# A graph attention layer on one core: the mish ratio moves from PSUM to SBUF, and the fourth tile of four groups goes through TensorE

## The reference

```python
sent   = nodes[senders] @ Ws + bs
e_att  = sent + edges @ We + be
recv   = nodes[receivers] @ Wr + br
logits = sum over a head of mish(e_att + recv) * attn_w + attn_b      # mish(x) = x * tanh(softplus(x))
w      = softmax of logits over the edges of one receiver
out    = segment_sum(w * e_att, receivers)
x      = layernorm(x + out)
```

## Time and profile before

| | |
|---|---|
| median of 3 runs | 3876.78 us (3872.36 to 3880.77) |
| the profiled execution | 3882.45 us, its span 3880.6 us |
| mean granted TensorE clock | 0.747 |
| busy: PE, DVE, ACT, POOL | 1900.8, 1878.8, 1681.8, 1552.4 us |

### The profile page before, as it was taken

The page is one execution under the profiler, slowest core; times in us unless marked ns, Lnnn a source line. Parts: engine busy times, 40 slices in busy tenths (PEclk is TensorE's granted clock), DMA queues, the critical chain, the costliest instruction groups (busy, mean ns, idle before and its releaser), DMA issues.

```text
span 3880.6 us, 49688 instructions
## 1 busy us (share of the span) xinstructions
PE 1900.8 (49%) x15454; PEld 1818.1 (47%) x15454; DVE 1878.8 (48%) x4399; ACT 1681.8 (43%) x2921; POOL 1552.4 (40%) x1640
## 2 busy tenths in 40 slices
PE   3345534544553553454364355356445445435536
PEld 3345534533543553454354355355445445435536
DVE  2435544544543554454465355445445445445537
ACT  0335534533543453453354354345335445435435
POOL 3443353344344334334434434433433543443440
PEclk8777777876876787787677677677668777767868
DMA  6111221211211121121121212212112112111220
GB/s 183 54 57 47 75 61 49 74 58 54 69 58 58 46 76 58 52 72 58 54 71 56 58 51 73 58 49 75 58 52 71 59 56 71 58 56 47 76 59 10
DMA packets 107469, 240.31 MB, mean 62 GB/s; under 512 B 46429, under 2 KB 73300, under 8 KB 100412
## 3 DMA queue, kind: packets, MB, share of 16 engines
q0 software_dynamic: 52224, 107.06, 10.5%
q1 hardware_dynamic: 53074, 132.41, 9.9%
q10 hardware_dynamic: 2142, 0.49, 0.1%
HBM read 230.09 MB, written 9.74 MB: 62 GB/s over the span
## 4 chain that ended last, share of the span: by engine, by line
another core or an unknown queue 32%; PE 26%; issue 21%; DVE 17%; ACT 1%; ACTq 1%; DVEq 1%
PE ps_z L785 7%; PE ps_z L786 6%; PE ps_sum L819 6%; DVE tbuf L1163 3%; DVE tbuf L1142 3%; DVE Z L1124 3%; DVE onehot L1113 2%; PE ps_edgeT L766 2%; DVE tbuf L1135 2%; PE ps_onehotT L771 2%; PE ps_ends L808 2%; PE ps_ends L800 1%; DVE Z L1232 1%; PE ps_ends L827 1%
## 5 line engine op out<-in xcount | busy, mean ns | idle before, releaser
L694 POOL DMA_INDIRECT gath<-xs_table,src_i x1632 | 1551.4, 951 | 2234.7 <-DVE Z L1124 1239.6
L785 PE MATMUL ps_z<-we_sb,edgeT 128*128 128x128 f32 x3264 | 722.5, 307 | 1545.7 <-ACT edgeT L909 888.2
L785 PEld LDWEIGHTS ps_z<-we_sb,edgeT 128*128 128x128 f32 x3264 | 564.8, 217 | 1569.6 <-ACT edgeT L909 904.0
L1124 DVE TENSOR_TENSOR Z<-ps_z,gath 128x512 f32<-128x512 f32 x408 | 280.9, 688 | 1616.5 <-remote 1076.6
L909 ACT COPY edgeT<-ps_edgeT 128x512 f32<-128x512 f32 x408 | 238.7, 585 | 1550.8 <-remote 1390.9
L786 PE MATMUL ps_z<-xr_buf,onehotT 128*128 128x128 f32 x3264 | 705.3, 302 | 0.0
L786 PEld LDWEIGHTS ps_z<-xr_buf,onehotT 128*128 128x128 f32 x3264 | 568.9, 218 | 0.0
L819 PE MATMUL ps_sum<-Z,onehot 128*128 128x132 f32 x3264 | 446.2, 286 | 17.0 <-issue 12.5
L819 PEld LDWEIGHTS ps_sum<-Z,onehot 128*128 128x128 f32 x3264 | 403.3, 195 | 15.3 <-issue 10.6
L940 ACT ACTIVATE ps_ratio<-tbuf,c_ln 128x512 f32<-128x512 f32 x408 | 281.8, 691 | 188.8 <-issue 120.3
L916 ACT CAST onehotT<-ps_onehotT 128x512 f32<-128x512 bf16 x408 | 240.6, 590 | 247.9 <-remote 122.0
(11 more groups left out here) (113 smaller groups left out, 1695.0 us busy)
## 6 DMA issues: line engine op xcount, KB each, us to landing
edge_buf<-in_edge_attr_dram SPq DMA_DIRECT2D x51, 2048.0 KB, 7.9
gath<-xs_table,src_i POOLq DMA_INDIRECT x1632
xr_buf<-xr_table SPq DMA_DIRECT2D x51, 64.0 KB
xr_in<-xr_table SPq DMA_DIRECT2D x51, 64.0 KB
x_in<-in_x_dram SPq DMA_DIRECT2D x51, 64.0 KB
out_dram<-y_out SPq DMA_DIRECT2D x51, 64.0 KB, 1.6
xs_table<-onehot SPq DMA_DIRECT2D x2, 896.0 KB
xr_table<-Z SPq DMA_DIRECT2D x1, 1568.0 KB
```

The source lines that it names most:

```text
L694: nc.gpsimd.indirect_dma_start(gath[:, b, t, :], None, xs_dram, bass.IndirectOffsetOnAxis(ap=src_i[:, b, t:t + 1], axis=0))\
L785: nc.tensor.matmul(ps_z[q][:, j, :], edgeT[:, q, j, :], we_sb[:, :], start=True, stop=False)
L1124: nc.vector.tensor_tensor(Zv[:, b, a:a + n, 0:D], ps_z[g % 2][:, 0:n, :], gath[:, b, a:a + n, :], ALU.add).then_inc(z_ready, 1)
```

## The change

The ratio's last step writes in place to tbuf in SBUF, and its wait for the mish before goes. The bank that this frees takes the heads' logits, so that ps_ends can hold four transposed tiles. TURN_T becomes 4: all tiles of the turned groups go through PE, 16 of 32. `score` and `reduce_heads` are left out for the turned groups, and their semaphores count plain groups alone. The first sum_heads of a window waits until the window before has been read.

```diff
-TURN_T = 3
+TURN_T = 4
+PLAIN = [g for g in range(NG) if g not in TURNED]
...
-        ps_ratio = ps("ps_ratio", [P, GT * D])
+        ps_heads = ps("ps_heads", [P, 512])
...
-        ps_logit = ps_ends[:, TURN_T * P:TURN_T * P + len(TURNED) * TURN_T * H]
+        ps_logit = ps_heads[:, 0:len(TURNED) * TURN_T * H]
...
             def sum_heads(w, g):
 
                 pe.wait_ge(mishT_ready, at_turned(w, g))
+                if g == TURNED[0]:
+                    wait(pe, heads_read, w)
...
                     act.wait_ge(ln_done, at(w, g))
-                    wait(act, mish_ready, at(w, g) - 1)
-                    nc.scalar.activation(ps_ratio[:, 0:GROUPS[g][1] * D], tb, ACT.Exp, bias=c_ln2[:, 0:1],
-                                         scale=-1.0).then_inc(ratio_ready, 1)
+                    nc.scalar.activation(tb, tb, ACT.Exp, bias=c_ln2[:, 0:1], scale=-1.0).then_inc(ratio_ready, 1)
...
-                ratio = ps_ratio[:, 0:n * D].rearrange("p (t d) -> p t d", d=D)
-                nc.vector.scalar_tensor_tensor(out=tb, in0=ratio, scalar=1.0, in1=Zv[:, b, a:a + n, 0:D],
+                nc.vector.scalar_tensor_tensor(out=tb, in0=tb, scalar=1.0, in1=Zv[:, b, a:a + n, 0:D],
...
+            def at_plain(w, g):
+
+                return w * len(PLAIN) + PLAIN.index(g) + 1
...
-                dve.wait_ge(scored, at(w, g))
+                dve.wait_ge(scored, at_plain(w, g))
...
-                dve.wait_ge(logit_ready, at(w, NG - 1))
+                dve.wait_ge(logit_ready, at_plain(w, PLAIN[-1]))
...
-                    if there(w0):
+                    if there(w0) and g0 in PLAIN:
                         score(w0, b0, g0)
                     aside(w, b, k, g, 2)
-                    if there(w0):
+                    if there(w0) and g0 in PLAIN:
                         reduce_heads(w0, b0, g0)
```

## The result

The changed kernel takes 3898.54 us (median of 5 runs, 3890.88 to 3915.84) against 3876.78 us (5 runs, 3872.36 to 3884.72): a ratio of 1.0066, 95% interval 1.0042 to 1.0090; the medians are 22 us apart. Forecast were 3914 us and "slower" at 0.72: the change is slower, and the forecast size, 37 us, was 15 us too large.

The account below looks back on a forecast made before the run. The bound was taken to be a loop of waits between gather batches, with PE setting the pace between release and add 7. PE 30, ends 2 and POOL 4 made +36 us: 3914 us against the 3876.78 median, range 3872 to 3945.

Parts of the forecast that it names:

- The loop and its three parts: Gather batches 74.4 us apart: 45.1 us to the stall's release, 14.4 to group 7's add, 16.3 to the next gathers.
- The PE term: Between release and add 7, two more tiles at 0.313 us each, 0.63 us a window: +30 us over 48 windows.
- rival C: No change: DVE's earlier one-hots get group 5 through in the shadow in nine more windows, giving back 36 us: 3878; chance 0.12.
- The shadow takes what DVE enters later: During the gather batch's stall: PE's beat becomes 4.66 us, DVE enters 0.14 us later or a little more, cost 0.
- The ends: First and last windows, without a gather to hide behind: about 2 us more.
- DVE's saving and ACT's added work at 0: In turned groups: DVE's 0.56 us less gains 0 where it waits for PE; ACT's added work is hidden under PE.
- POOL's +4 us: Gathers beside mishes that now read two SBUF operands: +4 us, between bounds of 0 and 49 us.
- The signs to look for: L800 and L808 counts 816 and 1632, 1.25 us per group, release to add 7 15.0 us, distance 75.1, PE-caused DVE idle above 420.2.
- B: Faster: DVE is the pace after the release and loses 1.2 us a window, -58 us: 3819; chance 0.10.
- F: The loop hides PE's tiles, for instance because the edge load and not add 7 starts the gathers: 3878; chance 0.07.
- E: Fewer windows get group 5 through in the shadow, DVE being 0.14 us later: 20 us more, 3934; chance 0.13.
- D: POOL held by every mish beside it: 49 us on top of 32, 3958, or 82 us, 3991; chance 0.08 together.

Follow-up runs that it names:

- e11: Kernel before with groups 3, 4 and 5 turned in place of 2 to 5, three tiles each: 3850.64 us against 3879.98, ratio 0.9926.
- first pair: Profiles of the kernel before and the changed kernel from the main comparison, measured at 3876.78 and 3898.54 us.
- second pair: Profiles of the kernel before (e9) and the changed kernel (e10), taken on one chip with the stall: 3879.77 and 3893.41 us.
- e9: The kernel before, unchanged, profiled on the chip whose loop has the stall: 3879.77 us in one run.
- e10: The changed kernel, run beside the kernel before on the chip with the stall: 3893.41 us against 3879.98, ratio 1.0039.
- e1: Changed kernel with three tiles through PE again, ratio still in SBUF, on a chip without the stall: 2220.97 us against the kernel before's 2150.52, ratio 1.0326.
- e2: Changed kernel with the heads' products issued twice in groups 2 and 3, on a chip without the stall: 2206.49 us, ratio 1.0252 to the kernel before.
- e3: Changed kernel with the heads' products issued twice in groups 4 and 5, on a chip without the stall: 2201.65 us, ratio 1.0233 to the kernel before.
- e12: e11 with DVE's normalisation moved ahead of group 6's mish, score and reduction: 3862.48 us against the kernel before's 3872.43, ratio 0.9990.

## Why the prediction was right, and where it missed

**The loop and its three parts: right.** The stall ends 45.1 us after the first gather, the part behind add 7 is unchanged to 0.03 us, and most of the difference stands where PE has the pace. e11 shows this from the other side: PE's work taken out of that part comes back, 29 us for a forecast of 27. One detail was misread: the chain isn't PE's alone from the release on. Its first 1.2 us are ACT's copy of the edge features (L909, 0.59 us) and 0.6 us of issue, which the fourth tile doesn't touch.

**The PE term: mechanism right, size too large.** Forecast were 0.63 us a window, 30 us in all. It is 0.35 and 0.34, some 16 us. The term that was mis-sized is "two tiles on the path" at "the plain price". The tile between adds 6 and 7 is there in full, 4.35 to 4.68 in nearly every window, 0.33 for the forecast 0.313. That between adds 5 and 6 shows only in small part: without the windows in which group 5 gets through, 4.91 to 4.96 in the first pair and 4.86 to 4.96 in the second. From release to add 7 those windows grew by 0.45 (13.80 to 14.25) and by 0.59 (13.40 to 13.99), the second near the forecast. What makes the second pair's mean 0.34 all the same is rival C's mechanism: six windows in place of four get group 5 through, and each then takes 4 to 5 us less, 0.2 us in the mean. Whether the change brings that about or chance, two profiles can't tell.

For the tile that hardly shows there is a likely reason. I had reckoned that the lower clock behind the release might double a tile's price; the rows show no such thing. PE runs at the lower of its two clocks (1.2 GHz, granted 0.50) for some 5.3 us behind the release in the kernel before and 4.9 with the fourth tile, in the second pair for 5.0 and 4.7. 0.3 to 0.5 us less of half speed is 0.15 to 0.25 us of work, about what is missing between adds 5 and 6 (0.26 and 0.21). But single windows differ by more than 1 us in this, and no run tested it: the reason is argued, not shown, and why the clock came back sooner the rows don't say.

**The shadow takes what DVE enters later: right.** Add 7 to add 0 went from 4.44 to 4.68 or 4.78 us (forecast 4.66). DVE so enters 0.3 us later and not the forecast 0.14, because its own beat was taken as 4.52, from a piece of the chain that begins after the add does. PE now paces it: DVE idles 0.97 us before add 7 in place of 0.38, and 0.2 us before add 0 where it had none.

**The ends: right.** The tail grew by 1.8 and 2.0 us for a forecast of about 2.

**DVE's saving and ACT's added work at 0: right.** The 50 us less of DVE's work show nowhere in the loop, where DVE idles longer before adds 6 and 7 than before, and e11, which gives work back to DVE, loses nothing by it. ACT's ratio takes 721 ns into SBUF and its copy 567 (forecast: 722 and at most 613), and neither line is in the chain between release and add 7:

```profile
L942 ACT ACTIVATE tbuf<-tbuf,c_ln 128x512 f32<-128x512 f32 x408 | 294.1, 721 | 5.0
...
L1142 DVE SCALAR_TENSOR_TENSOR tbuf<-tbuf,Z 128x512 f32<-128x512 f32 x408 | 279.3, 684 | 0.5 <-ACT tbuf L942 0.4
...
L925 ACT COPY mishT<-ps_ends 128x512 f32<-128x512 f32 x204 | 115.6, 567 | 32.2 <-remote 32.1 <-PE ps_ends L801 0.2
```

**POOL's +4 us: right for this chip.** The gathers take 4.8 and 5.0 us more, and the first part of the loop grew by 0.12 and 0.08 us, 5.5 and 3.7 us over 46 windows. So it is on the path, as forecast, and about a fifth of the result. That the sum met is partly luck: 138 gathers with a mish beside them take 0.067 us more each, 9 us, twice the forecast, and the others 0.003 us less each, 4 us.

**The signs to look for**: counts (816, 1632) and per-group times (1.28 for 1.25) were as said; the distance became 74.88 and 74.68 us for a forecast 75.1, release to add 7 13.6 and 13.4 in the mean and 14.1 in the window shown, for 15.0. The idle time of DVE caused by PE should have risen from 420.2; it is 381.9, though in 249 places in place of 198, and e9 and e10 have 509.3 and 464.8. That sum holds stalls of up to 20 us that a window's luck puts under PE or under "remote", so it says nothing of a cost of 0.3 us. And the prediction's "nine" short distances are eight, the ninth is 73.7 us; group 5 gets through in six windows, not nine.

**The rivals.** B fell (DVE is not the pace: it still idles before the adds of groups 6 and 7), and F (the tiles are not hidden; its time should have read 3884, as the tiles are 30 of the 36 us and not all of them). C and E can't be told from chance: group 5 gets through in 6 windows and 6, or in 4 and 6, the short distances are 8 and 6, or 8 and 7, and two profiles of the kernel before differ by as much (6 and 4). D fell for this chip, 5 us in place of 49. For a chip without the stall it is the whole story of e1, 70 us. That this lies between D's two prices of 49 and 82 is luck: D counted 120 mishes beside gathers, e1 has 470 gathers with one beside them, each held far less.

**What stays open:** what holds PE's results back during a batch on one kind of chip and not on the other; what the changed kernel costs on the other kind (its neighbours e2 and e3 lie 2.5 and 2.3% above the kernel before); and e1, e2 and e3 in the loop with the stall. So the split of the 22 us there, some 16 for PE and 5 for POOL, rests on the rows of four profiles and on e11, and not on an experiment that makes one of the two parts alone.

## What to carry to other kernels

When a loop has a stretch in which all engines wait for something they can't hasten, only the work between its end and the next trigger counts: moving 50 us from an idle-most-of-the-time DVE to PE costs what lands on PE's list in that stretch, and moving 27 us of it away (e11, one constant, 0.74% faster than before) gains about that much (29 us measured). Before freeing a PSUM operand, look at what runs on POOL beside its reader: the same instruction from SBUF made the indirect gathers beside it 0.07 to 0.15 us longer, 5 us in all where DVE stood still during most of them and 70 where it didn't. A trigger that is made earlier was worth nothing here, because the work that it shut out had to be done behind the release (e12).

## What the runs showed of the hardware

One program, the kernel before, took 3877 to 3880 us on one kind of chip and 2147 to 2151 on another. On the first kind the add that is stuck during a batch starts only 45.1 us after its first gather (1892.10 to 1937.16), although PE's record of the products that it waits for ends at 1904.08, 33 us before; on the second DVE follows PE at once, in the middle of a batch:

```profile
1004.05 0.69 DVE L1125 TENSOR_TENSOR Z<-ps_z,gath 128x512 f32<-128x512 f32 x1 [0.30 <-PE ps_z L787]
```

This is e1. The mean granted clock is 0.96 to 0.99 of full speed there, 0.74 to 0.76 on the first kind, where PE drops to 0.50 in each stall. An estimate for this kernel is worth little before it is known which of the two it is for.
